# Graph kernel: ranking stream with two sets of one-hots, rank-by-destination sums inside it, count pass with one matmul per column

## The reference

```
edge_index = stack([src, dst])
x = layernorm(x + L0(x, edge_index))                      # 2 x gcn_conv
x = layernorm(x + L1(x, edge_index))                      # GAT, 4 heads
x = layernorm(x + L2(x, edge_attr_3, edge_weight1, ...))  # attention, 8 heads
x = layernorm(x + L3(x, edge_index))                      # message layer
```

## Time and profile before

| what | value |
|---|---|
| runs shown | 15492.6, 15510.65, 15525.46 us |
| profiled execution, its time | 15500.2 us |
| its span (first to last instruction) | 15498.4 us |
| mean granted TensorE clock | 0.671 |
| PE busy | 11328.4 us (73%) |
| DVE busy | 8762.0 us (57%) |
| POOL busy | 6938.9 us (45%) |
| ACT busy | 3743.4 us (24%) |

### The profile page before, as it was taken

The page is one execution under the profiler, slowest core; times in us unless marked ns, Lnnn a source line. Parts: engine busy times, 40 slices in busy tenths (PEclk is TensorE's granted clock), DMA queues, the critical chain, the costliest instruction groups (busy, mean ns, idle before and its releaser), DMA issues. The chain is left out here.

```text
span 15498.4 us, 263663 instructions
## 1 busy us (share of the span) xinstructions
PE 11328.4 (73%) x46351; PEld 7994.1 (52%) x46352; DVE 8762.0 (57%) x33002; ACT 3743.4 (24%) x12262; POOL 6938.9 (45%) x7336
## 2 busy tenths in 40 slices
PE   7988888446666359775777779999567777577587
PEld 5666666236666224432222239999544444466444
DVE  4444444858888810126777766666555555566601
ACT  0122222002222000006888862222111111111100
POOL 0277777047777710005777750000077777444200
PEclk9855555665555579888999985555555555566598
DMA  0000000016676547655444452222155555433164
GB/s 25 1 2 2 2 2 2 0 50 197 199 198 195 146 163 269 221 185 109 108 108 107 108 87 63 63 63 63 41 158 156 156 156 156 106 100 100 47 247 167
DMA packets 1812376, 1676.61 MB, mean 108 GB/s; under 512 B 271444, under 2 KB 1664048, under 8 KB 1773712
## 3 DMA queue, kind: packets, MB, share of 16 engines
q1 hardware_dynamic: 1291008, 1199.97, 25.4%
q0 software_dynamic: 234960, 339.86, 10.0%
q10 hardware_dynamic: 286272, 135.29, 3.0%
HBM read 1160.30 MB, written 514.00 MB: 108 GB/s over the span
## 5 line engine op out<-in xcount | busy, mean ns | idle before, releaser
L1408 POOL DMA_INDIRECT acc<-tab_kv,idx x1664 | 1589.3, 955 | 2578.6 <-POOLq L2121 2058.7
L1408 POOL DMA_INDIRECT room<-tab_h,idx x1664 | 1587.0, 954 | 2104.8 <-POOLq L2121 1575.4
L882 POOL DMA_INDIRECT by_dst<-x,h x1568 | 1704.6, 1087 | 1015.7 <-POOLq L2121 537.7
L1487 PE MATMUL banks<-acc,room 128*128 128x512 f32 x3328 | 1642.5, 617 | 535.1 <-ACT acc L1437 391.8
L1489 PE MATMUL banks<-room 128*128 128x132 f32 (+1 forms) x6656 | 1720.2, 415 | 276.5 <-DVE room L1502 230.0
L1437 ACT ACTIVATE acc<-ident,room 128x128 f32<-128x128 f32 x5824 | 1747.0, 387 | 449.9 <-DMA room<-tab_h,idx 425.3
L882 POOL DMA_INDIRECT by_src<-big,h x1568 | 1517.1, 968 | 606.8 <-issue 449.6
L1502 DVE TENSOR_SCALAR room<-ramp,loc 128x128 f32<-128x128 f32 x6656 | 1751.7, 309 | 24.0 <-issue 22.5
L1489 PEld LDWEIGHTS banks<-room 128*128 128x128 f32 x6656 | 1462.6, 302 | 469.4 <-DVE room L1502 196.2
L1487 PEld LDWEIGHTS banks<-acc,room 128*128 128x128 f32 x3328 | 571.4, 191 | 1605.4 <-issue 1480.7
L1455 PE MATMUL banks<-ident,room 128*128 128x128 f32 x3328 | 1091.0, 430 | 315.0 <-DVE room L1502 311.0
(11 more groups left out here) (423 smaller groups left out, 17334.9 us busy)
## 6 DMA issues: line engine op xcount, KB each, us to landing
big<-cells SPq DMA_DIRECT2D x262, 1568.0 KB, 6.4
cells<-acc SPq DMA_DIRECT2D x1985, 64.0 KB, 1.5
cells<-acc ACTq DMA_DIRECT2D x1984, 64.0 KB
head_rows<-room SPq DMA_DIRECT2D x416, 264.0 KB, 3.2
room<-head_rows SPq DMA_DIRECT2D x416, 264.0 KB, 2.8
acc<-w_rows SPq DMA_DIRECT2D x208, 512.0 KB
value_rows<-acc SPq DMA_DIRECT2D x416, 256.0 KB, 2.8
room<-value_rows SPq DMA_DIRECT2D x416, 256.0 KB, 2.8
```

Source lines behind the costliest of these rows:

```text
L882: pool.indirect_dma_start(self.target, bass.IndirectOffsetOnAxis(self.slots[:, t:t + 1], axis=0), self.rec[:, t, :], None).then_inc(self.s ...
L1408: pool.indirect_dma_start(far[:, m % BODY, 0:row], None, table, bass.IndirectOffsetOnAxis(k.idx[:, m:m + 1], axis=0)).then_inc(k.gathered[ ...
L1487: last = pe.matmul(k.psum[G * (j % MAX_RING) + t][:, :], oh, rhs, start=True, stop=True)
```

## The change

Count: the two one-hots that share a stationary or moving side are joined. The destination block (50) becomes the stationary operand, and source block and low part lie side by side as one moving operand of 178 (`BOTH`), so that there is one matmul a column. The sums come out turned, so they are copied to SBUF once and transposed back.

Stream: the one-hots have two sets, made a round ahead; `turn` and `spread` of the next round's group 0 are issued in group 3. The 50 sums of `Rank` stand in the rounds 2 to 51, after the ranks of group 2. The small instructions at a round's end have three links fewer (a link is a wait for the instruction before).

```diff
-def one_hots(dve, k, out, row, width):
+def one_hots(dve, k, out, row, width, first=0):
...
+BOTH = NB1 + P
...
-                    one_hots(dve, k, hots[r][0], k.shi_bf[:, at], NB1)
-                    one_hots(dve, k, hots[r][1], k.dhi_bf[:, at], NB1)
-                    one_hots(dve, k, hots[r][2], k.dlo_bf[:, at], P).then_inc(made, 1)
+                    one_hots(dve, k, hots[r][0], k.dhi_bf[:, at], NB1)
+                    one_hots(dve, k, hots[r][1], k.shi_bf[:, at], NB1)
+                    one_hots(dve, k, hots[r][1], k.dlo_bf[:, at], P, NB1).then_inc(made, 1)
...
             dve.wait_ge(summed, 1)
+            dve.tensor_copy(by_to, counts).then_inc(drained, 1)
+            dve.wait_ge(turned, 1)
...
-                        to = column(hots[r][1], m, NB1)
-                        pe.matmul(cells, column(hots[r][0], m, NB1), to, start=False, stop=False,
-                                  skip_group_check=True)
-                        last = pe.matmul(degrees, column(hots[r][2], m, P), to, start=False, stop=False,
-                                         skip_group_check=True)
+                        last = pe.matmul(counts, column(hots[r][0], m, NB1), column(hots[r][1], m, BOTH),
+                                         start=False, stop=False, skip_group_check=True)
...
+            pe.wait_ge(drained, 1)
+            pe.transpose(cells, by_to[:, 0:NB1], k.ident[0:NB1, 0:NB1])
+            pe.transpose(degrees, by_to[:, NB1:BOTH], k.ident[0:NB1, 0:NB1]).then_inc(turned, 1)
...
     # Stream.vector
-            dve.wait_ge(self.added, i * ROUND_COLUMNS + 1)
-            one_hots(dve, k, self.hot_s, k.shi_bf[:, at], NB1)
-            one_hots(dve, k, self.hot_d, k.dhi_bf[:, at], NB1).then_inc(self.made, 1)
-            dve.wait_ge(self.made, i + 1)
...
+                if g == 0 and not last:
+                    dve.wait_ge(self.added, i * ROUND_COLUMNS + 1)
+                    make_hots(i + 1, 1 - r)
+                if g and count:
+                    count(g)
                 dve.wait_ge(self.looked, i * ROUND_COLUMNS + g * 4 + 4)
...
+        with dve.Fori(1, 1 + NB1 // 2) as i:
+            link.loop(i - 1, 6)
+            body(i * 2, 0, False, False, lambda g: g == 2 and rank.count(dve, i * 2 - 2))
+            body(i * 2 + 1, 1, False, False, lambda g: g == 2 and rank.count(dve, i * 2 - 1))
...
     # Stream.tensor
-            pe.wait_ge(self.made, i + 1)
-            turn(i, 0, first)
-            spread(i, 0, first)
             for g in range(4):
                 if g < 3:
-                    turn(i, g + 1, first)
+                    turn(i, r, g + 1, first)
                     spread(i, g + 1, first)
+                elif not last:
+                    pe.wait_ge(self.made, i + 2)
+                    turn(i + 1, 1 - r, 0, False)
+                    spread(i + 1, 0, False)
...
     # Stream.scalar
+                elif m == 12 and not last:
+                    copy_turn(i + 1, 0, False)
...
     # Rank
+    def count(self, dve, b):
+        k = self.k
+        dve.wait_ge(self.counted, b)
+        dve.tensor_scalar(k.mask, k.dhi, k.ramp[0:EP, bass.ds(b, 1)], 0.0, ALU.is_equal, ALU.add,
+                          accum_out=self.cnt[0:EP, bass.ds(b, 1)]).then_inc(self.counted, 1)
...
-        with dve.Fori(0, NB1) as b:
-            link.loop(b, 1)
-            link(dve, dve.tensor_scalar(k.mask, hi, k.ramp[0:EP, bass.ds(b, 1)], 0.0, ALU.is_equal,
-                                        ALU.add, accum_out=cnt[0:EP, bass.ds(b, 1)]))
-        link.end(NB1)
-        dve.sem_inc(self.counted, 1)
         dve.wait_ge(self.summed, 1)
...
     # rank_phase, TensorE
             incidence.tensor(pe)
+            pe.wait_ge(incidence.used, len(incidence.loads))
             rank.tensor(pe)
```

More of the change, by code:

```diff
@@ L366, in pairs @@
     return row.rearrange("p (o i) -> p o i", i=2)
-def one_hots(dve, k, out, row, width):
+def one_hots(dve, k, out, row, width, first=0):
     ramp = k.ramp_pair[:, 0:width, :].unsqueeze(1).to_broadcast([P, 8, width, 2])
-    return dve.tensor_tensor(out[:, :, 0:width, :], ramp, pairs(row).unsqueeze(2).to_broadcast([P, 8, width, 2]),
+    return dve.tensor_tensor(out[:, :, first:first + width, :], ramp, pairs(row).unsqueeze(2).to_broadcast([P, 8, width, 2]),
                              ALU.is_equal)
@@ L476, in __init__ @@
         room = k.chunk_room
-        self.hot_s, self.hot_d = (room[:, m * size:(m + 1) * size].bitcast(BF16)
-                                  .rearrange("p (o c i) -> p o c i", o=8, i=2) for m in range(2))
-        room = room[:, 2 * size:]
+        hots = [room[:, m * size:(m + 1) * size].bitcast(BF16).rearrange("p (o c i) -> p o c i", o=8, i=2)
+                for m in range(4)]
+        self.hot_s, self.hot_d = hots[0:2], hots[2:4]
+        room = room[:, 4 * size:]
         self.turn_sb = [room[0:NB1, m * 512:(m + 1) * 512] for m in range(2)]
@@ L492, in __init__, with vector, make_hots, body @@
         self.turn_bank, self.key_bank, self.look_bank = ps[1:3], ps[3:5], ps[5:7]
-    def vector(self, dve):
+    def vector(self, dve, rank):
         k, link = self.k, self.link
-        def body(i, first):
+        def make_hots(i, r):
             at = bass.ds(i * ROUND_COLUMNS, ROUND_COLUMNS)
-            dve.wait_ge(self.added, i * ROUND_COLUMNS + 1)
-            one_hots(dve, k, self.hot_s, k.shi_bf[:, at], NB1)
-            one_hots(dve, k, self.hot_d, k.dhi_bf[:, at], NB1).then_inc(self.made, 1)
-            dve.wait_ge(self.made, i + 1)
+            one_hots(dve, k, self.hot_s[r], k.shi_bf[:, at], NB1)
+            one_hots(dve, k, self.hot_d[r], k.dhi_bf[:, at], NB1).then_inc(self.made, 1)
+        def body(i, r, first, last, count=None):
             for g in range(4):
@@ L537, in tensor, with turn @@
                   skip_group_check=True).then_inc(self.added, 1)
-        def turn(i, g, first):
+        def turn(i, r, g, first):
             if not first or g >= 2:
@@ L543, in turn @@
                 last = pe.matmul(self.turn_bank[g % 2][0:NB1, u * P:(u + 1) * P],
-                                 column(self.hot_s, g * 4 + u, NB1), k.ident_bf[:, :], start=True, stop=True)
+                                 column(self.hot_s[r], g * 4 + u, NB1), k.ident_bf[:, :], start=True, stop=True)
             last.then_inc(self.turned, 1)
@@ L556, in spread, with body @@
             last.then_inc(self.spread, 1)
-        def body(i, first):
-            pe.wait_ge(self.made, i + 1)
-            turn(i, 0, first)
-            spread(i, 0, first)
+        def body(i, r, first, last):
             for g in range(4):
                 if g < 3:
-                    turn(i, g + 1, first)
+                    turn(i, r, g + 1, first)
                     spread(i, g + 1, first)
+                elif not last:
+                    pe.wait_ge(self.made, i + 2)
+                    turn(i + 1, 1 - r, 0, False)
+                    spread(i + 1, 0, False)
                 for m in range(g * 4, g * 4 + 4):
                     pe.wait_ge(self.table_copied, i * ROUND_COLUMNS + m + 1)
-                    pe.matmul(self.table, column(self.hot_s, m, NB1), column(self.hot_d, m, NB1), start=False,
+                    pe.matmul(self.table, column(self.hot_s[r], m, NB1), column(self.hot_d[r], m, NB1), start=False,
                               stop=False, skip_group_check=True).then_inc(self.added, 1)
@@ L576, in body @@
                               start=True, stop=True).then_inc(self.looked, 1)
-        body(0, True)
-        with pe.Fori(1, TURNS) as i:
-            body(i, False)
+        pe.wait_ge(self.made, 1)
+        turn(0, 0, 0, True)
+        spread(0, 0, True)
+        body(0, 0, True, False)
+        body(1, 1, False, False)
+        with pe.Fori(1, TURNS // 2 - 1) as i:
+            body(i * 2, 0, False, False)
+            body(i * 2 + 1, 1, False, False)
+        body(TURNS - 2, 0, False, False)
+        body(TURNS - 1, 1, False, True)
     def scalar(self, act):
@@ L588, in copy_turn, with body @@
             act.activation(self.turn_sb[g % 2], self.turn_bank[g % 2][0:NB1, :], ACT.Copy).then_inc(self.turn_copied, 1)
-        def body(i, first):
-            copy_turn(i, 0, first)
+        def body(i, first, last):
             for m in range(ROUND_COLUMNS):
@@ L919, in _ @@
             dve.tensor_copy(k.we2t[:, :], k.psum[7][:, 0:H2])
-            stream.vector(dve)
+            stream.vector(dve, rank)
             incidence.vector(dve)
```

51 lines of the change are left out of this document (30 added, 21 removed).

## The result

| | median, us | runs | ratio to the kernel before, 95% |
|---|---|---|---|
| before | 15518.06 | 4 (15492.6 to 15527.04) | |
| the change | 14784.03 | 4 (14754.14 to 14805.27) | 0.9527 (0.9514 to 0.9539) |
| forecast | 14805 (14720 to 14990) | | |

The change is 734 us faster. The profiled execution is the slowest of its four: 14805.27 us, with a span of 14803.5.

A forecast was written before the change was run, and what follows sets the result against it. TensorE was taken to bound the count pass, TensorE plus waits for VectorE's one-hots the stream, VectorE the rank loop. Gains of 272 + 310 + 116 = 698 us off 15500.2 gave 14802, stated as 14805 (14720 to 14990).

The forecast's parts named there:

- Count pass: One of two matmuls a column removed, the other moving 178 columns: 513 to 241 us, gain 272 (90 to 299).
- upper bound of 299: Largest gain allowed for the count pass, with VectorE making one-hots without any overhead in 214 us.
- the level case: Count pass: TensorE at 2.37 and VectorE at 2.40 us a round, nearly equal; 2.45 with waiting, 240 us in all.
- VectorE's 2.40: Count pass: three one-hots in 2.18 us a round, plus a loop's turn of 0.43 us every second round.
- The bound from below: Shortest count pass considered: VectorE without any overhead, 214 us.
- Stream: One-hots made a round ahead remove TensorE's 3.63 us wait; group cadence of 4.58 us then bounds it, gain 310 us.
- Rank loop: Rank by destination: its first loop is removed and its sums hide in the stream, gain 115.7 us.
- Rival 1: Stream: TensorE's clock rises without idle time, GpSimd's scatters then bound it; 229 us more gain, 14575 us; chance 8%.
- Rival 2: Count pass: weights aren't loaded beside the moving ones, 0.27 us a column, 423 us; 14985 us in total; chance 8%.
- Rival 3: Stream: sums or one-hots come late on VectorE and TensorE waits, up to 98 us; 14900 us; chance 10%.
- Rival 4: Stream: something else of VectorE's tail still ends the round, so the 310 us are lost; 15112 us; chance 4%.
- Rival 5: GpSimd's scatters, held up by VectorE at 2.85 us each, end the phase 1550 us later; 17050 us; chance 2%.

The follow-up runs named there:

- Experiment 1: Only the new count pass and its one-hots put into the kernel before, on a disturbed machine: 19741 us, ratio 0.9839, 313 us faster.
- Experiment 12: The whole change with the 50 sums back in a loop of their own behind the incidences, undisturbed: 14890.78 us, ratio 0.9593 to the kernel before.
- experiments 4, 8 and 11: The change with turns and spreads issued for two column groups at once: disturbed 0.9534, undisturbed 0.9510, with the scan's second operand also from PSUM 0.9437.
- the pairs: The change with the stream's transposes and spreads issued for two column groups at a time, undisturbed: 14749.93 us, ratio 0.9510 to the kernel before.
- experiment 5: The change with the first spread matmul of each key issued three times, disturbed: single run, 19866 us where the kernel before took 20336.
- the first six experiments: Variants of the change run while something outside slowed the machine: the kernel before took 20055 us beside the first four, 20336 beside the other two.

## Why the prediction was right

- **Count pass, 272 us forecast, 305 measured** (the first look's start; the matmuls run from 90.5 to 297.3 us). That one matmul a column halves TensorE's part and VectorE takes over was right; the size was too small, and the result lies just above the upper bound of 299. The engines weren't level, and both terms of "the level case" were off. TensorE's 2.37 us a round held only for the first two rounds; then the clock was at its higher level and 16 matmuls took 1.47 us. Had it stayed at the lower one, TensorE alone would have needed 98 x 2.37 = 232 us, and the gain could not have passed 281: some 24 us of it are a rise that the forecast counted as worth nothing. And VectorE's 2.40 was 2.10: the turn of the loop, which I took from the stream at 0.43 us, costs 0.42 once and then nothing. The bound from below (214 us) already was VectorE without overhead; it was the case to take, and overlapping instructions (three one-hots start 2.10 us apart, not 2.18) went under it. Experiment 1 gives 313 in time and 308 in its trace.
- **Stream, 310 forecast, 313 measured.** 4.57 us a group, 18.29 a round, no wait of TensorE for one-hots. What was next in line was the group cadence, as said. That the clock would keep no burst was right as well.
- **Rank loop, 116 forecast, 107 net.** The loop's 116 went; some 9 came back, 7 of them in the second loop, where the compare L873 lasts 1.20 us instead of 1.04 while scatters run (44 turns of it; from 2492 us on, the scatters over, it is back at 1.04). Before, no scatter was left by then. Experiment 12 prices its own, quicker loop at 96 us of the phase.
- **Rival 1, the clock rises in the stream (8%)**: false for this order. TensorE was busy 1789 of 1791 us at 0.50. The Trainium skill, page "TensorE: Matmul & The Clock Gate", section "Why this matters for your kernels", has continuous work without gaps give the full rate; this trace doesn't agree. Nor do the two count passes: before, TensorE was busy 513 of 515 us and its matmuls of 50 columns lasted as at the lower level throughout; now, with 178 columns each, it is idle 0.64 of every 2.10 us and keeps the higher one to the end. In the stream experiments 4, 8 and 11 have rises: the same matmuls, in rows of 24 wide ones. I had seen that in the bursts of the earlier trace rows and used it only to say that the bursts would go. The bursts that the change gave up and the 119 us that the clock brings the pairs both come behind such rows; that they have one cause is likely and not shown.
- **Rival 2, weights not hidden**: false. The weight loads (0.10 us each) run beside the matmuls, one per 0.148 and then 0.092 us.
- **Rival 3, sums or one-hots late**: false; in the stream TensorE waits 1.9 us for them in all, and experiment 12 prices the sums at nothing.
- **Rival 4, the seam stays**: false.
- **Rival 5, scatters held up by VectorE (2%)**: it didn't decide, but it was nearer than I had it. I forecast GpSimd done at 2351, 2444 at the worst; it was 2485. I had put the hold on the sums, which hold nothing: the pace beside them is 1.27 us. The one hold I had seen, 2.55 us, stood beside a cast of 2.40 us (L666), so length wasn't the sign to go by: a sum of 1.84 us holds nothing, a compare of 1.20 does. The instructions that hold it are the scan and the multiply of the second loop, which the scatters only reach because the change makes the ranking run ahead of them. I had the scatters' pace against the stream and never laid them beside what follows it. The Trainium skill has the rule, page "SBUF — State Buffer", section "SBUF: two separate sides": a VectorE operation with two SBUF inputs and a GpSimd operation that reads SBUF exclude each other for a whole instruction. The traces agree: 3.25 us beside the scan, 0.97 once one input is in PSUM. But the cast L666 and the compare L873 have one large input each and hold a scatter too.
- **Sum.** 305 + 313 + 107 = 726 us off the phase's end against 698 forecast; 15518 - 726 is 14792, and the median is 14784. The forecast of 14805 was 21 us above it, closer than its parts: the count pass was 33 us too small and the rank loop 9 too large, another 8 us of the median came from elsewhere, and against those 36 us in all (734 - 698) stands a time of before that was taken 15 us too low (14805 + 698 = 15503 for 15518). That part is luck.

## What to carry to other kernels

When a stage gets shorter, lay each engine that doesn't get shorter beside the stage that follows: it will still be at work there, next to other instructions. A wait of an engine off the path (537 us for GpSimd before, 68 after, none with the pairs) is a budget that each next change draws on, and once it is gone the gain stops there: 166 us in the stream were worth 33. An engine that is busy for the whole of a stage isn't yet at its best rate: another order of TensorE's work took 46 us off the stream at the same clock and 119 more by the clock.

## What the runs showed of the hardware

- TensorE's granted clock stayed at 0.50 (1.2 GHz) through 1791 us of unbroken work with transposes and spreads in rows of 12, and with rows of 20 in the disturbed stream of experiment 5; with rows of 24 it was 0.58 over the stream, spells of the higher level (2.4 GHz) coming behind 73 of the 195 rows looked at. Why behind some and not others, and whether the rows' length or their place in the round decides, wasn't told apart.
- In the change's count pass TensorE idled for 0.64 us of every 2.10 and stayed at the higher level for some 200 us.
- A matmul of 178 bf16 columns with 50 stationary takes 0.148 us at the lower and 0.092 us at the higher level, its weights loaded beside it.
- A held scatter ends some 0.8 us after the VectorE instruction that held it, whichever it is: 0.78 after the scan, 0.84 after the multiply, 0.83 after the compare (rows at 2189.92 to 2195.81), 0.84 after the cast before.
- The duration of an instruction on VectorE can depend on GpSimd too: the compare takes 1.20 us beside scatters and 1.04 without, in the change and in experiment 12.
- Under the disturbance of the first six experiments single waits across engines grew to 10 us and more at unchanged durations of the stream's instructions, and the kernel before took 4500 to 4800 us longer; the changes kept their sign and rank there. Times taken under it can only be compared with each other.
